# Pass 2 of a wavelet mixing layer: 64-row tiles, two arrangements of a spread image, six places

## The reference

```python
yl, yh = _dwt2(x, 4)                        # 12-tap filters, symmetric padding
yl_out = einsum('bixy,ioxy->boxy', yl, w_yl)            # 42 x 42 coefficients
yh_out = yh[:-1] + [einsum('bicxy,iocxy->bocxy', yh[-1], w_yh)]
return _idwt2(yl_out, yh_out)
```

## Time and profile before

| | us |
|---|---|
| median of 3 runs | 1979.89 (1979.47 to 1982.36) |
| the profiled execution | 1983.0 |
| its span | 1981.1 |
| PE busy in it | 1899.7 (96%) |
| DVE busy | 825.3 (42%) |
| ACT busy | 486.1 (25%) |
| moved by DMA | 827.12 MB, 417 GB/s of memory traffic over the span |

### The profile page before, as it was taken

How to read it: one execution, slowest core, us unless ns; L and a number is a source line. 1 busy time by engine, 2 the same in 40 slices (tenths; PEclk the granted TensorE clock), 3 DMA queues, 4 the chain that set the end, 5 groups by cost and what they waited for, 6 DMA issues and landing times.

```text
span 1981.1 us, 47583 instructions
## 1 busy us (share of the span) xinstructions
PE 1899.7 (96%) x19625; PEld 825.6 (42%) x19625; DVE 825.3 (42%) x931; ACT 486.1 (25%) x1060; POOL 72.7 (4%) x130
## 2 busy tenths in 40 slices
PE   8999999999999899999999999999999999999995
PEld 4666666666666554332232232232232232222221
DVE  2222222222222345555545555555545445445442
ACT  2233232332332551121121131121121121121110
POOL 1000000000000000000000000000000000000000
PEclk9999999999999999999999999999999999999998
DMA  9999999999999899999999999999999999999997
GB/s 383 405 408 414 412 422 421 421 422 422 422 422 422 338 406 381 420 421 430 429 430 429 431 429 431 430 431 430 430 429 429 430 431 431 430 431 431 430 432 303
DMA packets 80233, 827.12 MB, mean 418 GB/s; under 512 B 8912, under 2 KB 8912, under 8 KB 13520
## 3 DMA queue, kind: packets, MB, share of 16 engines
q1 hardware_dynamic: 62784, 575.10, 69.5%
q0 software_dynamic: 17424, 251.67, 29.9%
HBM read 558.29 MB, written 268.44 MB: 417 GB/s over the span
## 4 chain that ended last, share of the span: by engine, by line
PE 59%; DMA 36%; issue 2%; SPq 1%; DVE 1%; ACT 0%; DVEq 0%; POOLq 0%; ACTq 0%; POOL 0%
PE ps L578 27%; DMA x_sb<-x 19%; DMA out<-x_sb 16%; PE ps L419 10%; PE ps L549 8%; PE ps L432 5%; PE ps L565 3%; PE ps L510 1%; PE ps L505 1%; SPq L333 1%; PE ps L443 1%; DVE x_sb L854 1%; PE ps L451 1%; PE ps L539 1%; PE ps L465 1%
## 5 line engine op out<-in xcount | busy, mean ns | idle before, releaser
L854 DVE TENSOR_TENSOR x_sb<-ps,x_sb 128x1024 f32<-128x1024 f32 x292 | 354.9, 1223 | 348.4 <-PE ps L578 228.0
L578 PE MATMUL ps<-spread_sb,const 128*64 128x512 f32 x1920 | 438.9, 599 | 11.5 <-DVE x_sb L854 6.5
L578 PE MATMUL ps<-work,const 128*64 128x512 f32 x1920 | 438.9, 599 | 10.5 <-DVE x_sb L854 5.5
L854 DVE TENSOR_TENSOR work<-ps,work 128x1024 f32<-128x1024 f32 x220 | 267.3, 1223 | 255.9 <-PE ps L578 159.1
L419 PE MATMUL ps<-x_sb,const 32*32 32x512 f32 x8192 | 288.9, 601 | 23.1 <-DMA x_sb<-x 19.7
L549 PE MATMUL ps<-const,pick 128*84 128x512 f32 x514 | 277.1, 621 | 0.0
L432 PEld LDWEIGHTS ps<-const,work 128*128 128x128 f32 x2048 | 244.8, 192 | 51.8 <-ACT work L621 37.6
L578 PEld LDWEIGHTS ps<-spread_sb,const 128*64 128x64 f32 x1920 | 128.9, 138 | 312.8 <-issue 275.3
L578 PEld LDWEIGHTS ps<-work,const 128*64 128x64 f32 x1920 | 129.4, 139 | 311.3 <-issue 276.6
L432 PE MATMUL ps<-const,work 128*128 128x84 f32 x2048 | 253.9, 276 | 0.0
L621 ACT COPY work<-ps 128x512 f32<-128x512 f32 x256 | 131.4, 600 | 419.3 <-PE ps L419 419.3
(11 more groups left out here) (46 smaller groups left out, 529.9 us busy)
## 6 DMA issues: line engine op xcount, KB each, us to landing
x_sb<-x SPq DMA_DIRECT2D x256, 1024.0 KB, 10.1
x_sb<-x POOLq DMA_DIRECT2D x68, 2048.0 KB, 16.5
out<-x_sb SPq DMA_DIRECT2D x68, 2048.0 KB, 38.2
work<-x POOLq DMA_DIRECT2D x51, 2048.0 KB, 16.5
out<-work SPq DMA_DIRECT2D x51, 2048.0 KB, 36.0
work<-w_full SPq DMA_DIRECT2D x30, 896.0 KB, 7.5
out<-x_sb SPq DMA_DIRECT2D x9, 1024.0 KB, 7.4
work<-x SPq DMA_DIRECT2D x8, 1024.0 KB, 6.3
```

Source lines behind the costliest of these rows:

```text
L578: last = nc.tensor.matmul(ps[64 * h:64 * h + 64, 2 + k], const[:, SH + P * k + u:SH + P * k + P:2], spread(c - u + h), start=True, stop=True)
L854: nc.vector.tensor_tensor(part, ps[:, 2 + 2 * half:4 + 2 * half], part, ALU.add).then_inc(added[half], 1)
```

## The change

Six things, which belong together.

1. *Half axes.* The inverse matrix is banded. Output rows 0 to 255 need only coefficients 0 to 31 of each band, rows 256 to 511 only 10 to 41. So each half of an axis is a product over 64 numbers (2 bands of 32) instead of 84, kept on 64 partitions. `constants()` has the matrices in that form: `SW` (256 columns instead of 512), `SH` (4 x 64 columns instead of 4 x 128) and a new `SO` (2 x 64); the constants shrink from 1776 to 1392 columns.
2. *Picking.* `pick` is 128 x 128 per image; two copies of 128 x 64 take the two windows. `delta` holds the coefficients on 128 partitions (two windows of 64), and all transposes that fill it become `turn_step`: eight matmuls with 64 columns of weights, two side by side, instead of four transposes. `first_spread` goes: the first image is picked like the others.
3. *Two arrangements.* `spread_rows` computes the spread image twice, with its two halves on partitions 0 to 63 and 64 to 127, and the other way round: eight matmuls of 64 x 64 tiles and 256 columns, in two banks. Two copies of 128 x 512 bring it to SBUF. The banks for odd images are now 6 and 7, which they share with the coefficient steps; so these steps wait for each other in new places.
4. *Out.* A set of 128 output rows is two (`out_stage`) or four (`pair_stage`) matmuls with 64 rows. With both arrangements, neighbouring sets (k even and odd) use different rows of the array. The first 24 images (16 single, 8 in pairs) and the last 8 do so (`both=True` for pairs); in the batch loop all four sets read arrangement 0, and four tiles of 64 x 32 stand side by side.
5. *Loops.* The singles are a loop over 4 images, `turn2` over 8 becomes `fours` over 4. The coefficient steps of a batch come in the group of four before the last one of the batch, one pair of steps in images 0, 1 and 2. Three counters (`s_begun`, `o_begun`, `d_begun`) are incremented on TensorE before a set of matmuls.
6. *Places.* Six instead of seven; the room in `work` goes to the eight spread buffers. The last pair is place 5, in the last round.

```diff
-PLACES = 7
+PLACES = 6
-ROUNDS2 = PAIRS // PLACES
+ROUNDS2 = PAIRS // PLACES - 1
+WINDOW, SHIFT = 32, COEFS - 32
...
-SW, SH, EYE, NEG = 592, 1104, 1616, 1744
+SW, SH, SO, EYE, NEG = 592, 848, 1104, 1232, 1360
...
-            nc.gpsimd.memset(spread_sb[:], 0.0).then_inc(cleared, 1)
-            nc.gpsimd.memset(more_spread, 0.0).then_inc(cleared, 1)
...
+            def turn_step(step, bank):
+                for q in range(Q):
+                    for h in range(2):
+                        last = nc.tensor.matmul(ps[64 * h:64 * h + 64, bank, P * q:P * q + P],
+                                                step[:, ROWS * q + 2 * SHIFT * h:ROWS * q + 2 * (SHIFT * h + WINDOW)],
+                                                const[:, EYE:EYE + P], start=True, stop=True)
+                return last
...
-                for q in range(Q):
-                    last = nc.tensor.matmul(ps[0:ROWS, 6, P * q:P * q + P], first_stage[:, ROWS * q:ROWS * (q + 1)],
-                                            const[:, EYE:EYE + P], start=True, stop=True, is_transpose=True)
-                last.then_inc(d_done, 1)
+                turn_step(first_stage, 6).then_inc(d_done, 1)
...
+            def spread_rows(p, of):
+                for a in range(2):
+                    for half in range(2):
+                        to = 64 * (half ^ a)
+                        for h in range(2):
+                            part = slice(64 * h, 64 * h + 64)
+                            last = nc.tensor.matmul(ps[to:to + 64, 6 * p + h, 256 * a:256 * a + 256], of(part, half),
+                                                    const[part, SW:SW + 256], start=True, stop=True)
+                last.then_inc(s_done[p], 1)
...
-                nc.tensor.matmul(ps[0:ROWS, p], pick[:, p], const[:, SW:SW + SIZE],
-                                 start=True, stop=True).then_inc(s_done[p], 1)
+                pe.sem_inc(s_begun, 1)
+                spread_rows(p, lambda part, half: pick[part, p, 64 * half:64 * half + 64])
...
+            def out_stage(c, g):
+                p, n = c % 2, GROUP * g + c
+                pe.wait_ge(s_copied[p], 2 * g + c // 2 + 2)
+                for two in range(2):
+                    pe.wait_ge(added[two], n + 1)
+                    pe.sem_inc(o_begun[two], 1)
+                    for k in (2 * two, 2 * two + 1):
+                        for half in range(2):
+                            at = 64 * (half ^ (k % 2))
+                            last = nc.tensor.matmul(ps[64 * half:64 * half + 64, 2 + k],
+                                                    const[at:at + 64, SH + 64 * k:SH + 64 * k + 64],
+                                                    spread(c, k % 2)[at:at + 64], start=True, stop=True)
+                    last.then_inc(o_done[two], 1)
...
+            def pair_stage(c, g, both):
...
+                    for k in (2 * two, 2 * two + 1):
+                        a = k % 2 if both else 0
+                        of = SH + 64 * k if a == k % 2 else SO + 64 * (k // 2)
                         for h in range(2):
+                            for half in range(2):
+                                at, to = 64 * (half ^ a), 64 * h + 32 * half
+                                last = nc.tensor.matmul(ps[to:to + 32, 2 + k], const[at:at + 64, of + u:of + 64:2],
+                                                        spread(c - u + h, a)[at:at + 64], start=True, stop=True)
+                    last.then_inc(o_done[two], 1)
...
+            def fours(g, batch=None, both=False):
+                for c in range(GROUP):
+                    if batch is not None and c >= 2:
+                        pe.wait_ge(d_copied, STEPS * batch + IDLE + 1 + 2 * (c - 1))
...
+                    pair_stage(c, g, both)
+                    if batch is not None and c < STEPS // 2:
+                        coefs_stage(c, g, batch)
...
-                nc.scalar.copy(pick[0:ROWS, p], delta[0:ROWS, o]).then_inc(picked[p], 1)
+                for half in range(2):
+                    last = nc.scalar.copy(pick[:, p, 64 * half:64 * half + 64].rearrange("p (j b) -> p b j", b=BANDS),
+                                          window(delta[:, o], half))
+                last.then_inc(picked[p], 1)
...
-                nc.scalar.copy(spread(c)[0:ROWS], ps[0:ROWS, p]).then_inc(s_copied[p], 1)
+                for a in range(2):
+                    last = nc.scalar.copy(spread(c, a).rearrange("p (h w) -> p h w", h=2),
+                                          ps[:, 6 * p:6 * p + 2, 256 * a:256 * a + 256])
+                last.then_inc(s_copied[p], 1)
```

More of the change, by code:

```diff
@@ L529, in _ @@
             first_coefs(ROUNDS)
-            def coefs_stage(v, k):
-                pe.wait_ge(staged, STEPS * (k - 1) + v + 1)
-                pe.wait_ge(d_copied, STEPS * k + v + IDLE)
-                for q in range(Q):
-                    last = nc.tensor.matmul(ps[0:ROWS, 6 + v % 2, P * q:P * q + P],
-                                            stage[:, v, ROWS * q:ROWS * (q + 1)], const[:, EYE:EYE + P],
-                                            start=True, stop=True, is_transpose=True)
-                last.then_inc(d_done, 1)
@@ L558, in out_stage @@
-            def out_stage(c, t):
-                p, n = c % 2, SLOTS * t + c
-                pe.wait_ge(s_copied[p], SLOTS // 2 * t + c // 2 + 2)
-                for half in range(2):
-                    pe.wait_ge(added[half], n + 1)
-                    for k in (2 * half, 2 * half + 1):
-                        last = nc.tensor.matmul(ps[:, 2 + k], const[:, SH + P * k:SH + P * k + P], spread(c),
-                                                start=True, stop=True)
-                    last.then_inc(o_done[half], 1)
@@ L569, in pair_stage @@
-            def pair_stage(c, t):
-                u, n = c % 2, SLOTS * t + c
-                for h in range(2):
-                    pe.wait_ge(s_copied[h], SLOTS // 2 * t + c // 2 + 2)
-                for half in range(2):
-                    pe.wait_ge(added[half], n + 1)
-                    for k in (2 * half, 2 * half + 1):
-                        for h in range(2):
-                            last = nc.tensor.matmul(ps[64 * h:64 * h + 64, 2 + k], const[:, SH + P * k + u:SH + P * k + P:2],
-                                                    spread(c - u + h), start=True, stop=True)
-                    last.then_inc(o_done[half], 1)
@@ new lines, in _ @@
+            pe.wait_ge(cleared, 3)
+            spread_stage(0, 0)
+            with pe.Fori(0, SINGLE) as g:
+                for c in range(GROUP):
+                    if c < GROUP - 1:
+                        spread_stage(c + 1, g)
+                    else:
+                        spread_stage(0, g + 1)
+                    out_stage(c, g)
+            spread_stage(1, SINGLE)
+            with pe.Fori(SINGLE, FOURS_BATCH - 2) as g:
+                fours(g, both=True)
+            with pe.Fori(0, BATCH - 1) as k:
+                fours(FOURS_BATCH * k + (FOURS_BATCH - 2), batch=k + 1)
+                with pe.Fori(0, FOURS_BATCH - 1) as r:
+                    fours(FOURS_BATCH * k + r + (FOURS_BATCH - 1))
@@ L609, in _ @@
+            with pe.Fori(FOURS - 2, FOURS) as g:
+                fours(g, both=True)
         @block.scalar
@@ new lines, in _ @@
+            act.wait_ge(s_done[0], 1)
+            for a in range(2):
+                last = nc.scalar.copy(spread(0, a).rearrange("p (h w) -> p h w", h=2), ps[:, 0:2, 256 * a:256 * a + 256])
+            last.then_inc(s_copied[0], 1)
+            with act.Fori(0, SINGLE - 1) as g:
+                singles(g)
+            singles(SINGLE - 1, last=True)
+            pick_image(2, SINGLE)
+            copy_spread_pair(1, SINGLE)
+            with act.Fori(SINGLE, FOURS_BATCH - 2) as g:
+                fours(g)
@@ L802, in _ @@
+            with act.Fori(0, BATCH - 1) as k:
+                fours(FOURS_BATCH * k + (FOURS_BATCH - 2), batch=k + 1)
+                with act.Fori(0, FOURS_BATCH - 1) as r:
+                    fours(FOURS_BATCH * k + r + (FOURS_BATCH - 1))
+            with act.Fori(FOURS - 2, FOURS) as g:
+                fours(g)
         @block.vector
```

238 lines of the change are left out of this document (125 added, 113 removed).

## The result

The changed kernel takes 2002.19 us in the median of six runs (1999.13 to 2005.1), the kernel before 1980.12 us (1979.47 to 1982.36) beside it: a ratio of 1.011, 95% interval 1.0097 to 1.0123. It is slower by 22 us, where the forecast was 1978.2 us and 1974 to 1988.

What follows compares the result with a forecast made beforehand. The prediction took DMA, at 430 GB/s, as the bound. Gains of 1.2 us (start of pass 2) and 0.45 us (constants) took the median from 1979.9 to 1978.2 us; range for 8 in 10: 1974 to 1988 us.

Steps and rivals of the forecast that it cites:

- End. Unchanged: the one late DMA engine has its queue.: Kernel end: one late DMA engine's queue, some 10 us shorter with six places, still outlasts the adds; no change in time.
- 20 us are left: Batch loop: of 30 us of slack one place takes 9.75, leaving 20; nothing lost up to 4.79 us per image.
- DMA stays full without it: Ring of places: some 30 us of a place's round is waiting in a queue that DMA doesn't need to stay full.
- Six places cost nothing.: Ring of places: the round shrinks to 58.5 us, leaving 32 to 36 for a store where 15 sufficed; no cost.
- Rival 3: Ring of places: six are too few, 180 us more; a mild form costs up to 10 us (1988); chance 0.04.
- PE per image 4.67, coefficient pair 1.8.: Batch loop: an image takes PE 4.67 us instead of 4.61, a pair of coefficient steps 1.8 us instead of 0.90.
- rivals 1 and 4: Batch loop: PE becomes the bound, typically 2030 us, chance 0.13; row tiles take turns in a bank, 2720 us, chance 0.02.
- Coefficient pair costs nothing.: Batch loop: +2.7 us of PE per trip, making 154.8 us, still under DMA's 155.9 us; no time lost.
- Start of pass 2, 1.2 us.: Start of pass 2: DMA idle 1.2 us instead of 2.4, a gain of 1.2 us (bounds 0.5 and 2.4).
- the 0.45 us of the smaller constants: Pass 1: the second constants block shrinks from 1184 to 800 columns, a gain of 0.45 us, at least 0.
- Mixing hidden.: Mixing: each first_coefs grows by 0.4 us, hidden behind PE's waits for weights; 3.2 us if the cover failed.

Runs made afterwards that it cites:

- products cut in two: Kernel before, each product of 512 columns in its pairs' images cut into two of 256 columns: 1992.36 us (1.0054).
- SyncE: Kernel before, 50 spare semaphore increments in small loops behind each store of a pair on SyncE alone: 1996.01 us (1.0063).
- both idle engines: Kernel before, 50 spare semaphore increments in small loops behind each pair's store on SyncE and load on GpSimd: 2012.02 us (1.0155).
- half the products: Kernel before, pairs' images using the first images' stage, four products of 128x128 instead of eight of 128x64: 1976.96 us (0.9977).
- added to both edits: Kernel before with six places, plain coefficient steps and 15 spare increments in loops behind each store and load: 1998.8 us (1.0094).
- changed kernel, halved: Changed kernel, both arrangements in the batch loop, eight products of 64x64 an image in place of sixteen of 64x32: 1995.3 us (1.007).
- the half that was left out here: Changed kernel, batch loop's coefficient steps without the products for the lower 64 of 128 rows: 2004.04 us (1.011).

## Why the prediction was wrong

- **"End. Unchanged: the one late DMA engine has its queue."** This step failed. The prediction found that the kernel ends with one late engine's queue and then did not ask what makes it late. The engine falls behind, in pass 2, the faster the more instructions are executed. Cost in time per instruction, the difference of the ratios x 1981 us over the difference in instructions: 10.7 / 7680 = 1.4 ns (products cut in two), 12.5 / 8449 = 1.5 (SyncE), 30.7 / 16401 = 1.9 (both idle engines), -4.6 / -4064 = 1.1 (half the products), 12.3 / 4884 = 2.5 (added to both edits), 16.2 / 7392 = 2.2 (changed kernel, halved). The change has 18282 more: an estimate by these is 20 to 46 us, and 22 were measured, of which six places and the coefficient steps make some 6 by their own run. So the direction and the order of size are accounted for, not the 22 us to a few. This term was missing in the sum altogether.

  Shown: that time and lag follow the executed instructions in pass 2, in both directions and from three engines. The lag's growth per 100 us over the instructions in the trace per 100 us (900 to 1300 us) is 2.6 / 1186 = 2.2 ns before, 1.7 / 835 = 2.0 with half the products, 4.1 / 1842 = 2.2 cut in two, 4.2 / 1896 = 2.2 with SyncE's loops, 6.8 / 2636 = 2.6 with both, and 3.9 / 2534 = 1.5 after: in the same proportion the kernel before's own instructions would account for its own lag. Also shown: it doesn't hold in every stretch. In pass 1, from 200 to 600 us, there are 3999 instructions per 100 us at a DMA share of 1.01, and the last share of its 161 transfers lands at most 1.9 us behind the eighth; there nothing is stored.

  Open: by what path. The Trainium skill (Runtime: NRT & Kernel Launch, Instruction fetch mechanics) says that each sequencer fetches its code over a DMA queue of its own, and calls the cost of going from one block of code to the next mostly hidden. The traces agree: instructions have their own queues, and 30 more packets of TensorE's code cost nothing. So what the late engine does besides data is traffic or waiting that the profile doesn't list. One rival stands untested: each time here comes with a span and a granted clock that the profiler took, and a record kept of each instruction would be traffic of just this kind. No run was timed without it, so whether the loss is there in an execution that isn't recorded is open.
- **"20 us are left", "DMA stays full without it".** Wrong in kind. Of a store's 45.3 us the last 20 were the wait for one engine's share (lag at 1700 us: 19.8). The slack of the ring was the lag that it can bear, and it was being used up at 2.6 us per 100 us. The rate of 430 GB/s hid it, as all engines were full. That stores late in the run take 32.3 us, near the forecast 35, is luck: they took 30.3 at 900 us already, by the lag, where the forecast meant a queue that is shorter by a place.
- **Six places cost nothing.** The run has 1.0027, some 5 us; interval 3 to 7. Rival 3, at a chance of 0.04, has up to 10 us in its mild form. With the extra instructions six places also bring the limit nearer: 22 to 26 us of lag, where seven places bore 35.8.
- **PE per image 4.67, coefficient pair 1.8.** 4.59 and 1.90, both right; four tiles run at once, rivals 1 and 4 false. PE is busy for 190 of 200 us and the bound is elsewhere.
- **Coefficient pair costs nothing.** Nearly: 1.0013, and three quarters taken out of the changed kernel give 2 to 3 us.
- **Start of pass 2, 1.2 us.** The hole closed in full (1.01 for 0.71), the first store is issued at 748.28 (747.9 forecast). Its gain can't be seen under the rest, and neither can the 0.45 us of the smaller constants.
- **Mixing hidden.** Not quite: 404 GB/s in 690 to 736 us where the kernel before has 414, a matter of 46 x (1 - 404/414) = 1.1 us.
- The prediction's own first sign of being wrong, a trip's rate under 428 GB/s, was met, though for another reason than PE. The second, DVE waiting for PE more than for loads, was met on one tile and not on both together (37.7 and 45.9 us).

## What to carry to other kernels

Where DMA is the bound, look at how the sixteen shares of one transfer land before you call a long time to landing slack: if one engine is last each time, the kernel ends with it. Here each executed instruction more cost 1.1 to 2.5 ns of the kernel's time in the stretch that loads and stores at once, whether TensorE, SyncE or GpSimd had it, so smaller tiles that leave TensorE's time the same (18282 instructions more) cost more than the better start of pass 2 gave. Count executed instructions as a term of the sum for such a stretch, beside busy time and bytes, and look whether a shown lag of one engine supports it: pass 1 here had more of them and no lag. And before a run takes work out, ask whether that work ran beside other work: the half that was left out here had cost nothing.

## What the runs showed that was not expected

- Fifty semaphore increments per pair on each of two idle engines slow a DMA-bound kernel by 31 us in small loops and by 100 us written out, with DMA's share at 0.99 to 1.01 all the while: the share doesn't show it, GB/s does (412 in loops from 1500 to 1700 us and 388 written out, for 430). The share counts a packet that takes longer as busy: from 1500 to 1900 us in the loops' kernel the load packets still have a median of 611 ns, but one in twenty takes 964 or more.
- It need not be a single engine: with SyncE's loops alone a second one lags by 22 us at 1500, with the cut products by 12 us at 1900, and with six places and plain coefficient steps two go together at 12 us.
- With both arrangements in the batch loop TensorE is busy for three quarters of the time and its granted clock has a mean of 0.85 to 0.87, between its two levels of 1.2 and 2.4 GHz; the same number of instructions as in the changed kernel then takes 8 to 11 us more (by the ratios and by the medians). Why isn't settled.
- TensorE written out in full, 0.999, is as fast as in loops, while SyncE and GpSimd, with the increments written out and so some 375 instructions in a round, stand still for 5.2 to 6.7 us at each jump back.
